# Four small index buffers moved and the routed up-projection matrices padded to 384 columns each, in an S4D, routed-expert, attention and dense-expert block on one Trainium2 core

## The chip, the cores and the metric

The kernel runs on 1 core of a Trainium2 chip. The metric is the device time of one execution in microseconds (us). Before the change the median of 3 runs is 912.46 us (911.31 to 914.74).

## What is computed

The reference, cut to what matters here:

```python
xn = _layernorm(x)                                   # x: (4, 1024, 128)
x = x + _L0_attn_ref(xn, ...) + _L0_ffn_ref(xn, ...) # S4D long convolution + top-2 of 8 experts
xn = _layernorm(x)
x = x + _L1_attn_ref(xn, ...) + _L1_ffn_ref(xn, ...) # attention + 8 dense experts, gated

# _L0_ffn_ref: EMB_DIM 128, HIDDEN 341, 8 experts, TOP_K 2
h1 = einsum('bsd,ehd->bseh', x, W1); h2 = einsum('bsd,ehd->bseh', x, W2)
hidden = silu(h1) * h2
expert_out = einsum('bseh,edh->bsed', hidden, W3)

# _L1_ffn_ref: D 128, FF 512, 8 experts, every token through every expert
h = gelu(einsum('td,edf->etf', x, W1) + b1)
eo = einsum('etf,efd->etd', h, W2) + b2
```

All tensors are float32.

## The kernel before, in words

The program is written by hand: each engine has its own instruction stream, the streams are tied by semaphores, and nothing is ordered by a scheduler. Its stages, by the time of the profile:

1. Up to about 190 us: layer norm, routing of the 4096 tokens to two of eight experts each, the rows scattered to x_slots in device memory, and the S4D kernel and spectra.
2. 190 to 344 us, the routed experts: 19 chunks of 512 slots. For each chunk SyncE loads the expert's split up matrices (`up_load`, L511, tile wc), the down matrices (`down_load`, L514, tile wd) and the rows (`x_load`, L517, tile xc). TensorE turns the rows, multiplies them up (`up`, L1864), down (`down`, L1872) and turns the result back. In between VectorE does the Fourier products of the S4D part.
3. 344 to 384 us: back from the spectra (`positions`, z by prod) and the second layer norm.
4. 384 to 765 us, the dense experts: 8 groups of 512 tokens, 32 units of 128 hidden columns in each (`up1`, `down1`). A unit is six products on TensorE, two activations on ScalarE (L914, L915) and one subtraction on VectorE (L1683).
5. 765 us to the end: attention (`uv`, `scores`, `turn_probabilities`, `attend`).

Where precision is wanted the kernel splits a float32 operand into a high and a low part of type fp32r, and a product becomes three matmuls (`three`, L1766, its matmuls on L1769 to L1771): low by high, high by low, high by high. In a row of the profile `ps<-xt_hi,w_lo` means: the moving operand is xt_hi, the stationary operand (which a weight load puts into the array) is w_lo. The products of z by prod, hid by wd, and the transposes use plain float32.

The up matrices of the routed experts are split once, early: `w0_load` (L485) brings one expert's two matrices side by side to wraw, 128 partitions by WA = 2 * 341 = 682 columns; ScalarE rounds them into the high part of wc (`w0_high`), VectorE subtracts for the low part (`w0_low`, L1199), SyncE stores both to w0_split (L497). In wc each of two buffers holds high and low, 682 columns each, and in each of these the second matrix begins at column HID0 = 341. `up` takes pieces of 128, 128 and 85 columns of each matrix.

Buffers are laid one behind the other in SBUF in the order of their declaration, each rounded up to 32 bytes; a stage's buffers are given back when the stage ends, and later ones reuse the place. One piece of 128 fp32r columns is 512 bytes, so every slice that a product takes of a buffer begins at the same remainder modulo 512 bytes as the buffer, unless the buffer has rows that are no multiple of 512 bytes. From the declarations, the byte address modulo 512 in the kernel before:

```
w_hi, w_lo (dense experts, stationary)                    416
xt1_hi, xt1_lo, hid1_hi, hid1_lo (dense experts, moving)   32
xct_hi, xct_lo (routed up, moving)                        416
wc, buffer 0: high 32 / 372, low 200 / 28  (first / second matrix; stationary)
wc, buffer 1: high 368 / 196, low 24 / 364
hid (routed down, moving) 416; wd (stationary)            192
u_hi, u_lo (scores, moving) 416; xt1 (stationary)          32
pt_hi, pt_lo (attend, moving)                             416
v_hi, v_lo (attend, stationary)                           416
z (moving) and prod (stationary)                          256
ws_hi 128, ws_lo 192
```

The four index buffers next_row, next_gate, row_of and gate_of (32 bytes each, 128 together; GpSimd copies to and from them once per chunk) stand between yo and wst1 among the chunk buffers, so what is declared behind them lies 128 bytes further than what is declared ahead.

Of the kernel before, what the change touches and what calls it, by code (L numbers as in the profile page):

```python
# [16 lines left out]
P = 128  # L17
# [3 lines left out]
HID0 = 341  # L21
J0 = -(-HID0 // P)
# [6 lines left out]


NC = (2 * B * L - E) // W + E
WA, WD = 2 * HID0, J0 * P
MIN_PAIRS, MAX_PAIRS = (2 * B * L // W - 2) // 2, (NC - 3) // 2
SURE = 3 + 2 * MIN_PAIRS
assert NC % 2 == 1
# [55 lines left out]
def program(nc, x, state_params, log_dt, skip, ln_w, ln_b, wg0, w0, lag_row, prefix,  # L91
            dft_fwd, dft_inv, wqk_t, wv, wg1, gate_bias, w1_1, b1, w2_1, b2, out):
    ctx = ExitStack()
    with ctx:
        def sb(name, shape, dt=F32):
            return ctx.enter_context(nc.sbuf_tensor(name, shape, dt))
# [31 lines left out]
        mid1 = sb("mid1", [P, 3, T])  # L128
        mid1_mv = sb("mid1_mv", [P, T, 2])
        shift_col = sb("shift_col", [P, 1])  # L130


        phase = ExitStack()

        def tmp(name, shape, dt=F32):
            return phase.enter_context(nc.sbuf_tensor(name, shape, dt))
# [44 lines left out]
        hid = tmp("hid", [P, J0, W])  # L181
        yt = tmp("yt", [P, W])
        yo = tmp("yo", [P, 2, 4, P])
        next_row = tmp("next_row", [P, 2, 4], mybir.dt.int32)
        next_gate = tmp("next_gate", [P, 2, 4])
        row_of = tmp("row_of", [P, 2, 4], mybir.dt.int32)
        gate_of = tmp("gate_of", [P, 2, 4])
        wst1 = tmp("wst1", [P, STAGES, W])
        chunk_buffers, phase = phase, ExitStack()

# [1573 lines left out]
        def _(pe):  # L1764
            mm = nc.tensor.matmul

            def three(dst, a_hi, a_lo, b_hi, b_lo, first=True, last=True):

                mm(dst, a_lo, b_hi, start=first, stop=False)  # L1769
                mm(dst, a_hi, b_lo, start=False, stop=False)  # L1770
                return mm(dst, a_hi, b_hi, start=False, stop=last)  # L1771
# [92 lines left out]
            def up(q, s, j):  # L1864

                f, r = width0(j), (s + j) % 2
                for bank, col in ((r, 0), (2 + r, HID0)):
                    w = slice(col + j * P, col + j * P + f)
                    last = three(ps[0:f, bank], wc[:, s, 0, w], wc[:, s, 1, w], xct_hi[:, s], xct_lo[:, s])
                last.then_inc(up_done, 1)  # L1870
# [20 lines left out]
            def chunk_products(q, k, s, left, turn):  # L1891
                pe.wait_ge(hid_done, q * J0 + 1)
                up(q, s, 2)
                if not is_first(q):
                    turn_outputs(q - 1)
                down(q, k, s, 0)
                if left:
                    pe.wait_ge(hid_done, q * J0 + 2)
                    pe.wait_ge(xct_lo_done, q + 2)
                    pe.wait_ge(w_up_in[1 - s], (k + s + 1) * 16)  # L1900
                    up(q + 1, 1 - s, 0)
                down(q, k, s, 1)
                if left:
                    pe.wait_ge(hid_done, q * J0 + 3)
                    up(q + 1, 1 - s, 1)
                if left >= 2:
                    turn_inputs(q + 2, k + 1, s)
                down(q, k, s, 2)
# [246 lines left out]
def layout(a):  # L2155

    def by_state(p):

        return p.reshape(2, HH, N).transpose(0, 2, 1).reshape(P, HH)

    freq = np.concatenate([np.arange(0, HF, 2), np.arange(1, HF, 2)]) + 0.5
    place = np.arange(C).reshape(2, P, 2).transpose(2, 0, 1).ravel()
    angle = 2 * np.pi * np.outer(place, freq) / (2 * C)
    dft = np.stack([np.cos(angle), -np.sin(angle)]).astype(np.float32)
    fwd = dft.reshape(2, CT, P, HF).transpose(2, 1, 0, 3)
    inv = dft.transpose(0, 2, 1).reshape(2, HM, P, C).transpose(2, 1, 0, 3)
    tile, expert = np.divmod(np.arange(T * E), E)
    earlier = (tile[:, None] < tile) & (expert[:, None] == expert)
    prefix = np.concatenate([earlier, expert[:, None] == np.arange(E)], 1).astype(np.float32)
    d = dict(  # L2170
        x=a["L0_attn_x"],
        state_params=np.stack([by_state(a["L0_attn_" + n]) for n in ("log_A_real", "A_imag", "C_re", "C_im")], 1),
        log_dt=a["L0_attn_log_dt"], skip=a["L0_attn_D"], ln_w=a["L0_attn_ln_w"], ln_b=a["L0_attn_ln_b"],
        wg0=a["L0_ffn_Wg"].T,
        w0=np.concatenate([
            a["L0_ffn_W1"].transpose(0, 2, 1), a["L0_ffn_W2"].transpose(0, 2, 1),
            np.pad(a["L0_ffn_W3"].transpose(0, 2, 1), ((0, 0), (0, J0 * P - HID0), (0, 0)))
            .reshape(E, J0, P, P).transpose(0, 2, 1, 3).reshape(E, P, J0 * P)], 2),
        lag_row=np.concatenate([np.arange(LO), 2 ** np.arange(NB), E - np.arange(E), np.tril(np.ones((E, E))).ravel()]).astype(np.float32),
        prefix=prefix.reshape(2, P, T * E + E).transpose(1, 0, 2),  # L2180
        dft_fwd=fwd, dft_inv=inv,
        wqk_t=np.stack([a["L1_attn_W_query"].T, a["L1_attn_W_key"].T], 1),
        wv=a["L1_attn_W_value"],
        wg1=np.pad(np.concatenate([a["L1_ffn_Wg"], a["L1_ffn_Wt"]], 1), ((0, 0), (0, GW - E - 1))),
        gate_bias=np.pad(np.concatenate([a["L1_ffn_bg"], a["L1_ffn_bt"]]), (0, GW - E - 1)),
        w1_1=a["L1_ffn_W1"],
        b1=a["L1_ffn_b1"].reshape(E * J1, P).T,
        w2_1=a["L1_ffn_W2"],
        b2=a["L1_ffn_b2"].T,
    )  # L2190
    return {n: np.ascontiguousarray(v) for n, v in d.items()}
```

## Time and profile before

| what | value |
|---|---|
| median of 3 runs | 912.46 us (911.31 to 914.74) |
| the profiled execution's own time | 913.24 us |
| its span (first to last instruction) | 911.1 us |
| mean granted TensorE clock over the span | 0.928 of full speed |
| TensorE busy (PE) | 800.2 us, 88% |
| VectorE busy (DVE) | 642.5 us, 71% |
| ScalarE busy (ACT) | 573.1 us, 63% |
| GpSimd busy (POOL) | 184.3 us, 20% |
| moved by DMA | 82.16 MB |

The profiled execution lies 0.78 us above the median and 2.14 us above its own span. Matmuls overlap: a matmul's recorded duration (some 0.4 us for 512 columns) is longer than the time until the next one starts, so the cost of one matmul in a full stream is the distance between two starts, which the timeline shows. The granted clock is 1.00 for 2.4 GHz and 0.50 for 1.2 GHz.

### The profile page before, as it was taken

To read this page: it belongs to the slowest core of one execution; us is meant where nothing else is said; L and a number is where in the kernel's file an instruction comes from. 1 tells how busy PE (TensorE), PEld (TensorE's weight loads), DVE (VectorE), ACT (ScalarE), POOL (GpSimd) and SP (SyncE) were. 2 spreads that over 40 slices of the span, in tenths; PEclk is the share of its full clock that TensorE was granted. 3 is DMA by queue.
4 is the path that set the end of the run, shared out by engine and by line. 5 is a ranking of instruction groups with operands and counts; after the bars stand their busy time and mean duration, and the time that the engine had idled before them with its cause. 6 is when DMAs were issued, how large, how long until landed. Compare 5 with 4: busy or idle time off the path is not lost.

```text
span 911.1 us, 11973 instructions
## 1 busy us (share of the span) xinstructions
PE 800.2 (88%) x4082; PEld 620.1 (68%) x4082; DVE 642.5 (71%) x1472; ACT 573.1 (63%) x1022; POOL 184.3 (20%) x246
## 2 busy tenths in 40 slices
PE   6964317569999999699999999999999998999998
PEld 6522207446666664377788788878888887899997
DVE  6699205278885485696997889777777775877875
ACT  5840102125555554698987998799898986665564
POOL 0077770006776574000100000000000000000000
PEclk9976555779999999799999999999999999999999
DMA  8534325217777653132441121112121210000000
GB/s 265 204 133 140 122 76 159 66 43 230 230 244 217 195 184 104 23 85 55 102 81 39 37 58 47 40 42 49 47 46 47 47 47 0 8 18 12 19 18 24
DMA packets 79466, 82.16 MB, mean 90 GB/s; under 512 B 11248, under 2 KB 63728, under 8 KB 79152
## 3 DMA queue, kind: packets, MB, share of 16 engines
q1 hardware_dynamic: 68688, 67.98, 26.1%
q0 software_dynamic: 6496, 12.92, 5.5%
q10 hardware_dynamic: 4224, 0.52, 0.4%
q8 instruction: 32, 0.52, 0.2%
q14 instruction: 26, 0.21, 0.1%
HBM read 57.69 MB, written 23.70 MB: 89 GB/s over the span
## 4 chain that ended last, share of the span: by engine, by line
PE 56%; ACT 3%; DVE 3%; POOL 1%; issue 1%; DVEq 0%; ACTq 0%; POOLq 0%
PE ps L1769 17%; PE ps L1771 16%; PE ps L1770 16%; PE ps L2090 3%; PE ps L1954 3%; POOL y_rows L675 1%; ACT hid L914 0%; DVE hid_lo L1683 0%; PE ps L2116 0%; ACT L914 0%; ACT L892 0%; ACT hid_hi L915 0%; PE ps L1935 0%; ACT xn L885 0%; DVE stats L1410 0%
## 5 line engine op out<-in xcount | busy, mean ns | idle before, releaser
L1683 DVE TENSOR_TENSOR hid_lo<-hid,hid_hi 128x512 fp32r<-128x512 f32 x256 | 176.4, 690 | 76.9 <-ACT hid_hi L915 69.5
L914 ACT ACTIVATE hid<-ps,b_sb 128x512 f32<-128x512 f32 x256 | 177.7, 694 | 44.4 <-PE ps L1771 17.5
L915 ACT ACTIVATE hid_hi<-ps,b_sb 128x512 fp32r<-128x512 f32 x256 | 175.6, 686 | 0.0
L1769 PE MATMUL ps<-xt_hi,w_lo 128*128 128x512 f32 x256 | 104.3, 408 | 0.0
L1769 PE MATMUL ps<-hid_hi,w_lo 128*128 128x512 f32 x256 | 101.4, 396 | 1.9 <-DVE hid_lo L1683 1.8
L1771 PE MATMUL ps<-xt_hi,w_hi 128*128 128x512 f32 x256 | 102.1, 399 | 0.0
L1770 PE MATMUL ps<-hid_lo,w_hi 128*128 128x512 f32 x256 | 101.6, 397 | 0.0
L1770 PE MATMUL ps<-xt_lo,w_hi 128*128 128x512 f32 x256 | 100.9, 394 | 0.0
L1771 PE MATMUL ps<-hid_hi,w_hi 128*128 128x512 f32 x256 | 100.6, 393 | 0.0
L675 POOL DMA_INDIRECT y_rows<-yo,row_of x76 | 80.9, 1064 | 71.3 <-issue 66.9
L633 POOL DMA_INDIRECT x_slots<-xn,slot x64 | 68.1, 1063 | 63.3 <-DVE expert_of L1190 44.2
L720 ACT ACTIVATE prod<-ps 128x512 f32<-128x512 f32 (+1 forms) x18 | 10.5, 591 | 95.1 <-remote 63.6
L1769 PE MATMUL ps<-xct_hi,wc 128*128 128x512 f32 (+1 forms) x114 | 66.2, 581 | 3.3 <-DMA wc<-w_split 2.3
L1293 DVE TENSOR_TENSOR hid<-act,ps 128x512 f32<-128x512 f32 (+1 forms) x57 | 39.0, 684 | 39.9 <-ACT act L831 35.5
L831 ACT ACTIVATE act<-ps 128x512 f32<-128x512 f32 (+1 forms) x57 | 34.1, 598 | 52.5 <-PE ps L1771 42.6
L1769 PEld LDWEIGHTS ps<-hid_hi,w_lo 128*128 128x128 f32 x256 | 48.1, 188 | 16.0 <-DVE hid_lo L1683 5.5
L1879 PE MATMUL ps<-hid,wd 128*128 128x512 f32 (+1 forms) x114 | 58.0, 593 | 0.0
L1771 PEld LDWEIGHTS ps<-xt_hi,w_hi 128*128 128x128 f32 x256 | 48.4, 189 | 12.1
L1769 PEld LDWEIGHTS ps<-xt_hi,w_lo 128*128 128x128 f32 x256 | 48.6, 190 | 11.5
L1770 PEld LDWEIGHTS ps<-hid_lo,w_hi 128*128 128x128 f32 x256 | 48.1, 188 | 11.7
L1771 PEld LDWEIGHTS ps<-hid_hi,w_hi 128*128 128x128 f32 x256 | 48.1, 188 | 11.0
L1770 PEld LDWEIGHTS ps<-xt_lo,w_hi 128*128 128x128 f32 x256 | 48.6, 190 | 10.0
(332 smaller groups left out, 1720.2 us busy)
## 6 DMA issues: line engine op xcount, KB each, us to landing
gate_row<-gates_dram SPq DMA_DIRECT2D x64, 256.0 KB, 4.9
wc<-w_split SPq DMA_DIRECT2D x19, 682.0 KB
x_slots<-prod SPq DMA_DIRECT2D x11, 520.0 KB, 10.9
w_split<-wc SPq DMA_DIRECT2D x8, 682.0 KB
xc<-x_slots SPq DMA_DIRECT2D x19, 260.0 KB
wst<-w SPq DMA_DIRECT2D x16, 256.0 KB
wd<-w SPq DMA_DIRECT2D x19, 192.0 KB
acc<-y_rows POOLq DMA_DIRECT2D x14, 256.0 KB, 4.9
```

Source lines behind the costliest of these rows:

```text
L633: nc.gpsimd.indirect_dma_start(x_slots, bass.IndirectOffsetOnAxis(ap=slot[:, k, t:t + 1], axis=0), xn[:, t], None).then_inc(signal, 16)
L675: nc.gpsimd.indirect_dma_start(y_rows, bass.IndirectOffsetOnAxis(ap=row_of[:, s, t:t + 1], axis=0), yo[:, s, t], None).then_inc(y_stored[s ...
L831: nc.scalar.activation(act[0:f, r], ps[0:f, r], ACT.Silu).then_inc(act_done, 1)
L914: nc.scalar.activation(hid1[:, u % 4], ps[:, u % 4], ACT.Gelu_apprx_tanh, bias=b1_sb[:, u:u + 1])
L915: nc.scalar.activation(hid1_hi[:, u % 4], ps[:, u % 4], ACT.Gelu_apprx_tanh, bias=b1_sb[:, u:u + 1]).then_inc(hid1_done, 1)
L1293: tt(hid[0:f, j], act[0:f, r], ps[0:f, 2 + r], mul).then_inc(hid_done, 1)
L1683: tt(hid1_lo[:, u % 4], hid1[:, u % 4], hid1_hi[:, u % 4].bitcast(F32), sub).then_inc(hid1_lo_done, 1)
L1769: mm(dst, a_lo, b_hi, start=first, stop=False)
L1770: mm(dst, a_hi, b_lo, start=False, stop=False)
L1771: return mm(dst, a_hi, b_hi, start=False, stop=last)
L1879: last = mm(ps[:, 4], wd[0:f, s, j * P:(j + 1) * P], hid[0:f, j], start=(j == 0), stop=(j == J0 - 1))
L1954: last = mm(ps[:, g % 4], inv[:, m, part_, t * P:(t + 1) * P], z[:, m + HM * (t // 2), c, part_], start=(m == 0 and part_ == 0), stop=(m = ...
```

## The change

- The four index buffers are declared with the buffers that live through the whole program, ahead of all stage buffers, and no longer behind yo. Every stage buffer ahead of wst1 so lies 128 bytes further than before, and wst1 and wc lie where they did.
- Each of the two up matrices is padded from 341 to 384 columns with zeros in the input array: WA becomes 768 columns, the second matrix begins at column 384 (HALF0), and wc, wraw, w0_split and the rows of the input w0 grow with it. A row of w0 for one expert and partition grows from 1066 to 1152 floats.
- The products keep their sizes: `up` still takes 128, 128 and 85 columns.

Byte addresses modulo 512 after the change:

```
w_hi, w_lo, xt1_hi, xt1_lo, hid1_hi, hid1_lo               32
xct_hi, xct_lo, hid, wd                                    32
wc, both buffers, high and low, both matrices              32
u_hi, u_lo, v_hi, v_lo, pt_hi, pt_lo                       32
z and prod                                                 96
ws_hi 128, ws_lo 192 (as before)
```

The order of instructions on every engine is the same before and after. The instructions that change are the eight ScalarE copies and the eight VectorE subtractions of `w0_high` and `w0_low` (682 to 768 columns), the eight DMAs to wraw (341 to 384 KB), the eight stores to w0_split and the 19 loads of wc (682 to 768 KB each). Apart from these only addresses differ.

```diff
 NC = (2 * B * L - E) // W + E
-WA, WD = 2 * HID0, J0 * P
+HALF0 = J0 * P
+WA, WD = 2 * HALF0, J0 * P
...
         shift_col = sb("shift_col", [P, 1])
+        next_row = sb("next_row", [P, 2, 4], mybir.dt.int32)
+        next_gate = sb("next_gate", [P, 2, 4])
+        row_of = sb("row_of", [P, 2, 4], mybir.dt.int32)
+        gate_of = sb("gate_of", [P, 2, 4])
...
         yo = tmp("yo", [P, 2, 4, P])
-        next_row = tmp("next_row", [P, 2, 4], mybir.dt.int32)
-        next_gate = tmp("next_gate", [P, 2, 4])
-        row_of = tmp("row_of", [P, 2, 4], mybir.dt.int32)
-        gate_of = tmp("gate_of", [P, 2, 4])
         wst1 = tmp("wst1", [P, STAGES, W])
...
                 f, r = width0(j), (s + j) % 2
-                for bank, col in ((r, 0), (2 + r, HID0)):
+                for bank, col in ((r, 0), (2 + r, HALF0)):
                     w = slice(col + j * P, col + j * P + f)
...
         w0=np.concatenate([
-            a["L0_ffn_W1"].transpose(0, 2, 1), a["L0_ffn_W2"].transpose(0, 2, 1),
+            *(np.pad(a["L0_ffn_" + n].transpose(0, 2, 1), ((0, 0), (0, 0), (0, HALF0 - HID0))) for n in ("W1", "W2")),
             np.pad(a["L0_ffn_W3"].transpose(0, 2, 1), ((0, 0), (0, J0 * P - HID0), (0, 0)))
             .reshape(E, J0, P, P).transpose(0, 2, 1, 3).reshape(E, P, J0 * P)], 2),
```

## Rows read from the trace of the kernel before

**Rows 1.** The page: engines' busy time, and the granted clock in 40 slices.
```profile
PE 800.2 (88%) x4082; PEld 620.1 (68%) x4082; DVE 642.5 (71%) x1472; ACT 573.1 (63%) x1022; POOL 184.3 (20%) x246
...
PEclk9976555779999999799999999999999999999999
```

**Rows 2.** Stretches: start:end length, busy us (instructions) per engine, granted clock, DMA, GB/s.
```profile
240.00:300.00 60.00, 56.67 (x236) 36.72 (x235) 42.82 (x69) 32.35 (x72) 42.03 (x60) 1.00 0.78 231
300.00:344.00 44.00, 41.85 (x172) 27.12 (x171) 26.72 (x43) 23.84 (x55) 27.92 (x44) 1.00 0.63 193
...
384.00:765.00 381.00, 379.05 (x1688) 305.18 (x1688) 300.36 (x595) 332.80 (x529) 8.64 (x10) 1.00 0.24 52
765.00:911.10 146.10, 138.78 (x982) 126.40 (x982) 104.09 (x210) 84.21 (x160) 0.00 (x0) 0.99 0.05 15
```

**Rows 3.** The page: the chain that ended last, shares by engine.
```profile
PE 56%; ACT 3%; DVE 3%; POOL 1%; issue 1%; DVEq 0%; ACTq 0%; POOLq 0%
```

**Rows 4.** TensorE's waits from 380 to 766 us: us in total, times, longest.
```profile
PE ps L1769 <- DVE hid_lo L1683: 1.8, 4, 0.7
```

**Rows 5.** Timeline, dense experts, one unit of six products: start us, duration us, instruction.
```profile
700.39 0.40 PE L1769 MATMUL ps<-xt_hi,w_lo 128*128 128x512 f32 x1
...
701.79 0.40 PE L1769 MATMUL ps<-xt_hi,w_lo 128*128 128x512 f32 x1
```

**Rows 6.** Timeline, routed up at the start of its stage, six products apart.
```profile
192.59 0.63 PE L1769 MATMUL ps<-xct_hi,wc 128*128 128x512 f32 x1
...
195.15 0.63 PE L1769 MATMUL ps<-xct_hi,wc 128*128 128x512 f32 x1
```

**Rows 7.** The chain from 344 to 380 us: start us, us, what.
```profile
344.45 24.05 PE ps L1954 x56
```

**Rows 8.** Timeline, routed up of two neighbouring chunks, four products apart in each.
```profile
304.48 0.39 PE L1770 MATMUL ps<-xct_lo,wc 128*128 128x512 f32 x1
...
305.41 0.40 PE L1771 MATMUL ps<-xct_hi,wc 128*128 128x512 f32 x1
...
312.15 0.39 PE L1770 MATMUL ps<-xct_lo,wc 128*128 128x512 f32 x1
...
313.08 0.40 PE L1771 MATMUL ps<-xct_hi,wc 128*128 128x512 f32 x1
```

**Rows 9.** Timeline, attend, nine products apart.
```profile
851.77 0.29 PE L1771 MATMUL ps<-pt_hi,v_hi 128*128 128x256 f32 x1
...
852.85 0.28 PE L1771 MATMUL ps<-pt_hi,v_hi 128*128 128x256 f32 x1
```

**Rows 10.** Timeline, gate logits with 10 moving columns, nine products apart.
```profile
414.71 0.25 PE L1771 MATMUL ps<-ws_hi,xt_hi 128*128 128x10 f32 x1
...
415.71 0.25 PE L1771 MATMUL ps<-ws_hi,xt_hi 128*128 128x10 f32 x1
```

**Rows 11.** Tile wc: duration ns min/median/max, first and last start; who waited for it.
```profile
L720 ACT ACTIVATE wc<-wraw x8: 757/764/774, 43.8 to 144.5; 128x682 fp32r<-128x682 f32 x8
L1199 DVE TENSOR_TENSOR wc<-wraw,wc x8: 860/862/869, 55.7 to 145.5; 128x682 fp32r<-128x682 f32 x8
...
  PE ps L1769: 2.3, 2
```

**Rows 12.** The same operations at 512 columns: tile khat, and the page's costliest groups.
```profile
L720 ACT ACTIVATE khat<-ps x4: 597/597/598, 171.6 to 177.2; 128x512 f32<-128x512 f32 x4
...
L1683 DVE TENSOR_TENSOR hid_lo<-hid,hid_hi 128x512 fp32r<-128x512 f32 x256 | 176.4, 690 | 76.9 <-ACT hid_hi L915 69.5
```

**Rows 13.** Waits up to 190 us: us in total, times, longest.
```profile
PE ps L1834 <- DVE high L1272: 6.2, 1, 6.2
```

**Rows 14.** DMA issues of wc, count and KB each.
```profile
wc<-w_split SPq DMA_DIRECT2D x19, 682.0 KB
```

**Rows 15.** Timeline of ScalarE, dense experts, four activations apart.
```profile
600.93 0.69 ACT L914 ACTIVATE hid<-ps,b_sb 128x512 f32<-128x512 f32 x1
...
603.21 0.72 ACT L914 ACTIVATE hid<-ps,b_sb 128x512 f32<-128x512 f32 x1
```

## The prediction

> **What bounds the kernel now.** I read the page first, then the stretches, the chain, the waits, and last the timeline. The page gives TensorE 800.2 us of 911.1, and a clock at or near full speed from the dense experts on [rows 1]. The stretches show where that holds: 379.05 busy of 381.00 us in the dense experts, 138.78 of 146.10 in attention, some 95% in the routed experts [rows 2]. The chain that ended last has 56% on TensorE [rows 3], and in the dense experts TensorE waits 1.8 us for its partner [rows 4]. So from about 200 us on nanoseconds per matmul are the kernel's time, and the question is what a matmul costs above its columns.
>
> The timeline tells that by distances between starts. In the dense experts six products take 701.79 - 700.39 = 1.40 us, 233.3 ns each [rows 5]. The same kind of product at the granted 1.2 GHz takes (195.15 - 192.59)/6 = 426.7 ns [rows 6], which is 512 columns at one per cycle and nothing else. At 2.4 GHz that would be 213.3 ns. **Each fp32r product of 512 columns thus pays 20.0 ns over its stream, at the high clock only.** Plain float32 hardly pays: z by prod, 24.05/56 = 429.5 ns [rows 7], is two streams of 213.3 and 2.9 ns. Something in the fp32r stream, perhaps the reading of two operands at once from SBUF, costs 20 ns. The change can win only if that depends on how the two addresses stand to each other modulo 512.
>
> **The change part by part.**
>
> *Addresses.* What the 20 ns do with the remainder is shown by two places. Routed up [rows 8]: neighbouring chunks use the two buffers of wc, whose pieces lie at 372, 200, 28 and 368, 196, 24, 364 and so on against a moving operand at 416. That makes eight differences. Four products take 0.93 us in both, 232.5 ns each, as many as in the dense experts with their one difference of 384. So among unequal remainders it makes no difference which. Equal ones are different ground: of the fp32r products only attend has them today, at 416 and 416, with 256 columns. Nine take 1.08 us, 120.0 ns each [rows 9]; the stream is 256/2.4 = 106.7, the excess 13.3 ns. Its other floor is the weight load: with 10 columns a product still takes (415.71 - 414.71)/9 = 111.1 ns [rows 10]. So equal addresses do not bring attend to either floor, it is 8.9 ns above the higher one. I can't read from this whether its 13.3 is a smaller sum per product than 20.0 or a larger one per column. The products whose remainders become equal and which lie on TensorE's full stretches are 1536 in the dense experts, about 300 of the 342 in routed up (the first chunks are waited for), and 192 in the scores: 2028. Attend keeps equal remainders, at 32. The bounds: down to 213.3 + 1.5 (half of z by prod's 429.5 is 214.8), a gain of 18.5 ns, 2028 x 18.5 = 37.5 us; up, the excess of attend per column, 13.3 x 2 = 26.7 ns against 20.0, a loss of 6.7 ns or 13.6 us. I take 0, because the row nearest in kind and size, routed up against the dense experts, changes its difference and not its time, and because attend with equal addresses still pays.
>
> The Trainium skill (TensorE: Matmul & The Clock Gate, Part 2, step 1) says that TensorE has two independent SBUF read ports, one for the moving operand and one for weight loads, and that loading the next tile's weights does not steal from the running matmul. By that rule no remainder can matter and this term is 0, as I take it. The trace agrees in that eight differences cost the same, but not in the rest: the same page (Wait — 56ns, not 53.3ns?) has 512 columns at 215.7 ns, and the dense experts show 233.3 [rows 5]. If the 17.6 ns between came from a conflict that the page leaves out, the whole gain would be open.
>
> *Early splitting, 8 copies and 8 subtractions with 86 more columns.* ScalarE: (764 - 597)/(682 - 512) = 0.98 ns a column [rows 11, 12], so 84 ns more each. VectorE: (862 - 690)/170 = 1.01, so 87 ns more each. ScalarE idles around them. The first two subtractions stand on VectorE ahead of the tables that TensorE waits 6.2 us for [rows 13]: +0.17 us. The other six I cost at nothing, since VectorE idles next to four of them and TensorE is slowed by issue, not by tables, behind the other two; without that cover they cost 6 x 0.087 = 0.5 us.
>
> *More bytes.* 8 loads grow by 43 KB, 8 stores and 19 loads by 86 KB each [rows 14]. At the 231 GB/s of the busiest stretch [rows 2] 86 KB are 0.38 us. Before the chunks that is 8 x 0.19 + 8 x 0.38 + 2 x 0.38 = 5.3 us of transfer in all, from none to all of it on the way; I take 0.4 us, one transfer's lateness, since the transfers have gaps and the route to the first chunk runs over the S4D kernel. In the chunks the load of wc is issued when a chunk's last up product is done and needed more than a chunk later; TensorE waited for it twice, 2.3 us in all [rows 11]. Each of these two grows by 0.38: +0.8 us. The other end is that all 17 are late by it, 6.5 us. The DMA engines are busy to 0.78 in that stretch and go to about 0.82, not full.
>
> A sentence apart: the Trainium skill (DMA: Bandwidth & Descriptors, How a descriptor splits into AXI transactions) says that a transaction must begin at a multiple of 256 bytes and that a descriptor which doesn't start there fetches bytes it won't use. A row of 5456 bytes starts off such a multiple in most partitions, one of 6144 never, so by that page the loads would grow by 7 to 9% rather than 12.6%, and the 0.8 us by some 0.3 less. No run here shows it yet.
>
> *Index buffers.* Copies of 4 elements on GpSimd at another address: nothing, in either direction.
>
> Sum: 913.24 (the profiled execution) + 0 + 0.17 + 0.4 + 0.8 = 914.6; the median lies 0.78 lower: **913.8 us**, where a measurement of this kernel can tell about 0.5% (4.6 us) from no change.
>
> **The rivals.**
>
> *Equal remainders save a part (faster).* Then attend's 13.3 ns is the price of a product with equal remainders, whatever its columns, and 20.0 falls by 6.7 ns: 2028 x 6.7 = 13.6 us, 900.2 us. If only attend's 8.9 ns over its weight load counted, 11.1 ns would go, 22.5 us, 891.3. For it: 13.3 is less than 20.0, and the excess appears only at the high clock [rows 6], as it would where SBUF reads are the limit. Against: eight unequal differences, some within 52 bytes of equal (364 and 368 against 416), show no slope.
>
> *They save all of it (faster).* 37.5 us, 876.3. ScalarE would allow it: four activations in 2.28 us [rows 15] make 1.14 us a unit, less than 6 x 214.8 = 1.29. Against it is attend, which has equal remainders and an excess.
>
> *Equal remainders are the worst case (slower).* Both reads of a matmul then begin at the same place of the interleave, and attend's 13.3 ns at 256 columns become 26.7 at 512: +6.7 ns on each of the 2028, +13.6 us, 927.4. It decides from the point where the price grows with the columns. For it: attend pays 5.2 ns per 100 columns, the dense experts 3.9. Against: attend's weight load of 111.1 ns explains a part of its excess without any conflict.
>
> *The bytes come late (slower).* The wc loads run out of slack, all 5.3 + 6.5 us show: 913.8 + 4.9 + 5.7 = 924.4 at the most, some 919 if half does. Against: two waits in 19 loads.
>
> *The change doesn't do what it says.* The remainders are arithmetic on the declarations, so I give this nothing; a part of the products (gate logits and uv, with ws at 128 and 192) stays unequal, but has 216 matmuls and is left out of all cases.
>
> **How the numbers follow.** No effect of the addresses: 0.47, with its own range 911 to 918.5. A part saved: 0.31. All saved: 0.05. Worst case: 0.12. Late bytes: 0.05. Faster by over 0.5% is 0.31 + 0.05 = 0.36; slower 0.12 + 0.05 = 0.17; the same 0.47. The range takes in the first two with their ends and half of the late bytes, 890 to 920, and leaves out 0.05 + 0.12 + 0.02 = 0.19.
>
> **What the profile after would show.** If I am right, six products of a dense unit still take 1.40 us, the copies read some 848 ns and the subtractions 949, and the wait for wc grows from 2.3 to about 3 us. If a part is saved, a unit takes 1.36 us and the dense stretch is 10 us shorter; if equal is worst, 1.44 us. Attend must stay at 120.0 ns in every case but one: if it moves too, the effect is not the equality of remainders but the absolute address, 32 in place of 416, and my reading of attend as a witness for equality falls with it. A longer stretch before 190 us would be the bytes.

## The result, and the profile after

The changed kernel takes 906.19 us (median of 4 runs, 905.31 to 907.3) against 912.1 us before (4 runs, 911.31 to 914.74): a ratio of 0.9927, 95% interval 0.9908 to 0.9946. It is 0.7% or 5.9 us faster. The forecast was no change, 913.8 us; the time lies in the range of 890 to 920 and on the side that had 0.36.

The page of the changed kernel, whose profiled execution took 906.6 us: span, busy time, granted clock in 40 slices, the chain's shares, one group, one DMA row.

```profile
span 904.5 us, 11973 instructions
...
PE 794.2 (88%) x4082; PEld 621.3 (69%) x4082; DVE 643.0 (71%) x1472; ACT 574.0 (63%) x1022; POOL 183.9 (20%) x246
...
PEclk9976555769999999889999999999999999999999
...
PE 56%; ACT 3%; DVE 2%; POOL 1%; issue 1%; DVEq 0%; ACTq 0%; POOLq 0%
...
L1770 PE MATMUL ps<-xct_hi,wc 128*128 128x512 f32 (+1 forms) x114 | 65.7, 576 | 2.7 <-DMA wc<-w_split 2.5
...
wc<-w_split SPq DMA_DIRECT2D x19, 768.0 KB
```

Against [rows 1, 3] nothing changes places: the same count of instructions, the same 56% of the chain on TensorE. TensorE alone is 6.0 us less busy (800.2 to 794.2). The loads of wc have their 768 KB [rows 14].

Where it went, first by stretches of the changed kernel (columns as in [rows 2]):

```profile
240.00:300.00 60.00, 57.29 (x239) 36.85 (x238) 42.56 (x69) 32.72 (x73) 41.94 (x62) 1.00 0.80 244
...
384.00:757.00 373.00, 371.02 (x1686) 305.54 (x1686) 298.85 (x594) 332.50 (x527) 8.61 (x10) 0.99 0.25 53
757.00:904.50 147.50, 140.05 (x987) 127.08 (x985) 105.21 (x211) 84.68 (x161) 0.00 (x0) 1.00 0.05 15
```

The dense experts do the 1686 matmuls of [rows 2] (there 1688 in 381 us) in 373 us; attention takes what it took. Exactly, by the first product of the stage and the last start of the type that ends it. In the kernel before, the timeline row of the first product:

```profile
384.19 0.77 PE L1769 MATMUL ps<-xt_hi,w_lo 128*128 128x512 f32 x1
```

and tile w_hi (minimum/median/maximum in ns, first and last start in us):

```profile
L1771 PE MATMUL ps<-hid_hi,w_hi x256: 389/392/404, 389.6 to 763.1; 128*128 128x512 f32 x128
```

In the changed one, the same two:

```profile
384.55 0.77 PE L1770 MATMUL ps<-xt_hi,w_lo 128*128 128x512 f32 x1
```

```profile
L1772 PE MATMUL ps<-hid_hi,w_hi x256: 388/389/398, 390.4 to 756.3; 128*128 128x512 f32 x128
```

That is 379.0 us before and 371.8 after. **The dense experts win 7.2 us, and the whole span 6.6.** The rest is small and of both signs. The routed up products start at 190.8 in place of 191.2 us and take, to the start of the last one, 146.3 in place of 147.0; what follows up to the dense experts takes 47.4 in place of 46.0; attention and the end 148.2 in place of 148.0. The sum is -0.4 - 0.7 + 1.4 - 7.2 + 0.2 = -6.7.

What a product costs shows in a settled stretch, as the distance between two starts 60 products apart. Before:

```profile
459.61 0.40 PE L1769 MATMUL ps<-xt_hi,w_lo 128*128 128x512 f32 x1
...
473.61 0.40 PE L1769 MATMUL ps<-xt_hi,w_lo 128*128 128x512 f32 x1
```

After:

```profile
459.19 0.39 PE L1770 MATMUL ps<-xt_hi,w_lo 128*128 128x512 f32 x1
...
472.79 0.39 PE L1770 MATMUL ps<-xt_hi,w_lo 128*128 128x512 f32 x1
```

14.00 us against 13.60: **233.3 ns fall to 226.7**. The excess over the stream of 213.3 ns falls from 20.0 to 13.4 ns, and is not gone.

The low price is not there from a run's first product. The timeline of the changed kernel where a plain float32 transpose (ident, gates) has broken the run of fp32r products:

```profile
435.44 0.27 PE L1943 MATMUL ps<-ident,gates 128*64 128x128 f32 x1
435.47 0.48 PE L1770 MATMUL ps<-xt_hi,w_lo 128*128 128x512 f32 x1
435.79 0.40 PE L1771 MATMUL ps<-xt_lo,w_hi 128*128 128x512 f32 x1
...
436.94 0.39 PE L1770 MATMUL ps<-xt_hi,w_lo 128*128 128x512 f32 x1
...
438.30 0.39 PE L1770 MATMUL ps<-xt_hi,w_lo 128*128 128x512 f32 x1
...
441.02 0.39 PE L1770 MATMUL ps<-xt_hi,w_lo 128*128 128x512 f32 x1
```

The five from 435.79 to 436.94 take 230 ns each, the six to 438.30 226.7, the twelve to 441.02 again 226.7. Averaged over all breaks of the dense experts' stream the changed kernel has 232.7 ns in the first three intervals, 229.8 and 228.1 in the next two triples and 226.7 from the tenth product on; the kernel before has 230.9, 234.6, 231.8 and 233.2.

A break need not be a plain float32 matmul. The gate logits are fp32r products too, with 10 columns, and behind them the changed kernel starts dear again:

```profile
416.01 0.25 PE L1772 MATMUL ps<-ws_hi,xt_hi 128*128 128x10 f32 x1
416.12 0.49 PE L1770 MATMUL ps<-xt_hi,w_lo 128*128 128x512 f32 x1
416.44 0.40 PE L1771 MATMUL ps<-xt_lo,w_hi 128*128 128x512 f32 x1
...
417.84 0.39 PE L1771 MATMUL ps<-xt_lo,w_hi 128*128 128x512 f32 x1
```

Six distances in 1.40 us, 233.3 ns. Behind a wait of TensorE for hid_lo it is the same: 231 to 234 ns in the first three distances, 226.5 in the tenth. So what seems to count is how many products of 512 columns have followed each other without a gap.

Of the distances between dense products 1182 stand beyond the ninth of such a run: 1182 x 6.67 = 7.9 us, about the 7.2 won. The full balance is this: the mean distance of all neighbouring dense products, slow and waiting ones left out, falls from 233.0 to 227.4 ns, 8.2 us over 1457 of them. Some 0.5 us of it is lost in the stage's first fifteen products, more of which the changed kernel runs at the low clock, with starts 427 ns apart (6.12 us in place of 5.64), and 0.5 in the waits for hid_lo and at the stage's end, where a distance of 1140 ns becomes 1294 and one of 740 becomes 855.

So the products that come in short runs gain little. Over the last four distances of each run of six, a routed up product falls from 232.2 to 230.9 ns and one of the scores from 231.7 to 231.3. Routed up stands between plain float32 products. The scores mostly don't: 30 of their 32 runs come straight behind fp32r products of 256 or fewer columns, as here in the changed kernel behind attend:

```profile
785.36 0.28 PE L1772 MATMUL ps<-pt_hi,v_hi 128*128 128x256 f32 x1
785.48 0.40 PE L1770 MATMUL ps<-u_hi,xt_lo 128*128 128x512 f32 x1
...
786.64 0.39 PE L1772 MATMUL ps<-u_hi,xt_hi 128*128 128x512 f32 x1
```

Five distances in 1.16 us, 232 ns, with equal remainders and twelve fp32r products just before. Attend takes 119.0 and 119.5 ns on the mean, hid by wd 431.1 and 431.2.

Tile wc in the changed kernel shows the price of the padding:

```profile
L721 ACT ACTIVATE wc<-wraw x8: 827/838/846, 43.2 to 142.8; 128x768 fp32r<-128x768 f32 x8
L1200 DVE TENSOR_TENSOR wc<-wraw,wc x8: 949/950/957, 55.0 to 143.8; 128x768 fp32r<-128x768 f32 x8
```

The copies grew from 764 to 838 ns, the subtractions from 862 to 950 [rows 11], and the last subtraction still starts earlier than before (143.8, before 145.5).

Last, a loss that nobody ordered. At the end of the routed experts TensorE waits 2.2 us for yt, in both kernels. Before (the last number is the idle time before the row):

```profile
343.79 0.66 PE L1888 MATMUL ps<-ident,yt 128*128 128x128 f32 x4 [2.15 <-ACT yt L835]
```

and the 6 us around it, with columns as in [rows 2]:

```profile
340.00:346.00 6.00, 3.85 (x12) 1.64 (x11) 0.69 (x1) 2.24 (x6) 3.56 (x5) 1.00 0.69 259
```

After:

```profile
342.68 1.11 PE L1889 MATMUL ps<-ident,yt 128*128 128x128 f32 x4 [2.16 <-ACT yt L836]
```

```profile
340.00:346.00 6.00, 3.84 (x10) 1.97 (x9) 0.69 (x1) 2.24 (x6) 3.38 (x5) 0.72 0.52 180
```

The granted clock is 1.00 in these 6 us before and 0.72 after: once the wait is over the changed kernel runs at 1.2 GHz for a while. The transposes take 1.11 in place of 0.66 us, and z by prod behind them 28.7 in place of 27.6: 1.5 us in all, more than the 0.7 that the routed experts had gained.

### The profile page after: what moved, and what is told of

The parts are those of the page before. It is cut to its first block, busy times and chain, and to the rows that moved or that the text cites. A ratio compares the mean times of both kernels' runs of the same rounds, so it can differ in the third digit from the quotient of the medians.

```text
span 904.5 us, 11973 instructions
## 1 busy us (share of the span) xinstructions
PE 794.2 (88%) x4082; PEld 621.3 (69%) x4082; DVE 643.0 (71%) x1472; ACT 574.0 (63%) x1022; POOL 183.9 (20%) x246
## 4 chain that ended last, share of the span: by engine, by line
PE 56%; ACT 3%; DVE 2%; POOL 1%; issue 1%; DVEq 0%; ACTq 0%; POOLq 0%
PE ps L1770 17%; PE ps L1772 16%; PE ps L1771 16%; PE ps L2091 3%; PE ps L1955 3%; POOL y_rows L676 1%; ACT hid L915 1%; DVE hid_lo L1684 0%; ACT hid_hi L916 0%; PE ps L2117 0%; ACT L915 0%; ACT L893 0%; PE ps L1936 0%; ACT xn L886 0%; DVE stats L1411 0%
## 5 line engine op out<-in xcount | busy, mean ns | idle before, releaser
L1771 PE MATMUL ps<-hid_lo,w_hi 128*128 128x512 f32 x256 | 99.7, 389 | 0.0
L1835 PE MATMUL ps<-low,high 64*32 64x32 f32 x256 | 30.7, 236 | 30.0 <-issue 23.9
```

What stands on the lines that cost most here:

```text
L1835: mm(o, high[states, 0, c * CH + h], low[states, 0, c * CH + h], start=True, stop=False)
```

## The experiments

Two theories stood after the result. One: equal remainders make a product cheaper. The other: the absolute place does it (the weights went from 416 to 32), or some part of the change other than the dense experts' addresses. All ratios are against the kernel before on the same chip, with 95% intervals. The first four ran on a chip where the kernel before takes 872.04 us (14 runs, 868.85 to 873.31): its routed experts begin about 40 us earlier, the rest is alike, so only comparisons among the four and with that number are made. Stage lengths are from the first to the last start, as above.

**e1: the index buffers moved, no padding.**

```diff
+        next_row = sb("next_row", [P, 2, 4], mybir.dt.int32)
...
-        next_row = tmp("next_row", [P, 2, 4], mybir.dt.int32)
```

> Only the index buffers are moved; the up matrices stay at 682 columns. The dense experts' and the attention's operands all lie at 32, the routed up pieces stay unequal. Theory A (equal remainders of the moving and the stationary operand shorten long streams of fp32r products, so only the dense experts gain): dense stretch 372 us as after the change, steady 226.7 ns per product, time 905 to 906. Theory B (the padding, through the routed up, brings part of the gain): 908 or more.

865.51 us (863.94 to 866.39), ratio 0.9933 (0.9911 to 0.9956). Its timeline, 60 products apart:

```profile
418.72 0.39 PE L1769 MATMUL ps<-xt_hi,w_lo 128*128 128x512 f32 x1
...
432.32 0.39 PE L1769 MATMUL ps<-xt_hi,w_lo 128*128 128x512 f32 x1
```

13.60 us, 226.7 ns, and a dense stage of 371.4 us. The move of 128 bytes alone gives the whole gain.

**e2: the padding, the index buffers where they were.**

```diff
-WA, WD = 2 * HID0, J0 * P
+HALF0 = J0 * P
+WA, WD = 2 * HALF0, J0 * P
```

> Only the padding to 384 columns; the index buffers stay, so w at 416 against 32 in the dense experts as before. Theory A: dense stretch 379 us, 233.3 ns per product, and the time is 912 plus the price of the bytes, 912 to 914. Theory B: below 911.

874.04 us (872.76 to 877.43), ratio 1.0037 (1.002 to 1.0054). Sixty products take 13.95 us, 232.5 ns, the dense stage 378.4. The padding gives nothing and costs: the interval puts it at 1.7 to 4.7 us, the medians lie 2.0 apart. Of this its profile shows, against that of e1, 1.6 us before the first chunk (152.4 against 150.8) and 0.7 us in the routed experts.

**e3: the kernel before, with a gap of 384 bytes ahead of the dense experts' moving buffers.** Weights stay at 416, the moving operands come to 416 too.

```diff
+        gap1 = tmp("gap1", [P, 96])
         xt1_hi = tmp("xt1_hi", [P, G, W], F32R)
```

> The kernel before with a gap of 384 bytes ahead of xt1_hi: the dense experts' moving operands lie at 416, as w does. Equality as the cause: dense stretch 372 us, 226.7 ns, time 905. The absolute place as the cause (w at 32 is good, at 416 bad): 379 us, 233.3 ns, time 912.

864.46 us (864.07 to 865.79), ratio 0.9928 (0.9899 to 0.9957). Sixty products from 417.18 to 430.78 us, 226.7 ns; dense stage 371.5. The absolute place is out: both at 32 (e1, the changed kernel) and both at 416 are cheap, one at each is dear. So is a clash of one operand with some third buffer that stayed where it was: in this stage e1 moves the stationary operand alone and e3 the moving ones alone, and both win the same. It is the difference of the two addresses, and one unused buffer does what the change does. (The gap also moves hid1, the unrounded buffer that stands between the moving ones.)

**e4: the same with a gap of 128 bytes**, moving minus stationary 256 modulo 512.

> The kernel before with a gap of 128 bytes ahead of xt1_hi: moving operands at 160, w at 416, a difference of 256 in place of 128. If equality alone counts: 379 us and 233 ns, time 912. If the price goes with the difference, another steady distance than 233.3, between 226.7 and 240 ns, and a dense stretch between 371 and 390 us.

863.47 us, ratio 0.9914 (0.9886 to 0.9942). Its timeline:

```profile
416.21 0.39 PE L1770 MATMUL ps<-xt_hi,w_lo 128*128 128x512 f32 x1
...
429.81 0.39 PE L1770 MATMUL ps<-xt_hi,w_lo 128*128 128x512 f32 x1
```

226.7 ns again. So equality modulo 512 isn't the condition either; a difference of 256 does as well. From here on each difference is tried at one place only, with the stationary operand at 416.

**e5, e6, e7, e9, e10: gaps of 448, 352, 256, 64 and 416 bytes**, for differences of 64, 480, 384, 192 and 32. These ran on chips where the kernel before takes 913.54 (e5 to e8) and 913.05 us (e9 to e12).

> A gap of 448 bytes: moving at 480, stationary at 416, difference 64. If the price grows with the distance from a multiple of 256: between 226.7 and 233.3 ns, some 230, dense stretch 375 us. If only 128 modulo 256 is bad: 226.7 ns and 372 us. If every difference that is no multiple of 256 is bad: 233 ns and 379 us.

> A gap of 352 bytes: moving at 384, stationary at 416, difference 480 (-32), so that the two also stand at different places of a 64-byte block. If only multiples of 128 or 256 matter: 226.7 ns or a value between, 372 to 375 us. If the place within 64 bytes matters by itself: another steady distance than at 64, possibly above 233 ns or below 226.7.

> The kernel before with a gap of 256 bytes ahead of xt1_hi: dense moving operands at 288, w at 416, moving less stationary = 384 modulo 512 (-128). So far 0 and 256 gave 226.7 ns and 128 gave 233.3. If the remainder modulo 256 decides, 384 is as bad as 128: 233 ns, dense stretch 379 us, same time as before. If 128 alone is bad (a direction): 226.7 ns, 372 us, 0.8% faster.

> A gap of 64 bytes ahead of xt1_hi: moving at 96, stationary at 416, difference 192. Measured so far, steady ns: 0 and 256 226.7, 64 228.9, 128 and 384 233, 480 233.3. If the price repeats every 256 bytes and is the same on both sides, 192 is as 64: 229 ns, dense stretch 374.5 us. If it repeats but is not symmetric, 192 lies with its neighbours 128 and 480 (which is 224 modulo 256): 233 ns, 379 us.

> A gap of 416 bytes: moving at 448, stationary at 416, difference 32. If a start off the stationary operand's 64-byte grid is dear by itself, as 480 was: 233 ns, 379 us. If the price rises from 0 over 64 to 128: between 226.7 and 228.9 ns, some 373 us.

| kernel | moving - stationary, mod 512 | ns a product, over one settled stretch of 60 | dense stage, us | ratio |
|---|---|---|---|---|
| e3, e1, changed | 0 | 226.7 | 371.4 to 371.8 | 0.9928, 0.9933, 0.9927 |
| e10 | 32 | 233.3 | 379.2 | 1.0008 (0.9995 to 1.002) |
| e5 | 64 | 228.9 | 374.4 | 0.9923 (0.9906 to 0.994) |
| before | 128 | 233.3 | 379.0 | 1 |
| e9 | 192 | 233.3 | 380.1 | 1.0018 (1.0002 to 1.0034) |
| e4 | 256 | 226.7 | 372.0 | 0.9914 |
| e7 | 384 | 232.5 | 379.4 | 0.9979 (0.9956 to 1.0003) |
| e6 | 480 | 233.3 | 379.3 | 1.001 (0.9983 to 1.0037) |

The one between, e5, as its timeline has it:

```profile
460.42 0.39 PE L1770 MATMUL ps<-xt_hi,w_lo 128*128 128x512 f32 x1
...
474.15 0.39 PE L1770 MATMUL ps<-xt_hi,w_lo 128*128 128x512 f32 x1
```

13.73 us, 228.9 ns. Two differences give the full gain, 64 two thirds of it, and the rest none: a step of 32 bytes to either side of equal loses everything. The 232.5 of 384 is its stretch; over all products beyond the ninth it has 233.0, and before 233.2. What sets 64 apart is the stage's length and not the ratio, whose interval covers that of the full gain. No distance from a multiple of 256 orders the table: 32 costs more than 64, and 192, which is 64 below 256, more than 64 itself. As 320 and 448 weren't tried, the rule behind it stays open.

**e8: the changed kernel, with two chunks' up pieces next to each other.** If a run has to be longer than nine products to settle, twelve in a row should show it in the routed experts.

```diff
                     pe.wait_ge(w_up_in[1 - s], (k + s + 1) * 16)
-                    up(q + 1, 1 - s, 0)
                 down(q, k, s, 1)
+                if left:
+                    up(q + 1, 1 - s, 0)
```

> The changed kernel with the second down product of a chunk ahead of the first up piece of the next, so that two up pieces, 12 fp32r products, follow each other without a plain float32 product between. If a stream must run some 9 products before it settles at 226.7 ns, products 10 to 12 of these runs take 227 ns, where products of runs of six take 231 on average; gain at most 19 x 25 ns = 0.5 us, so the time is that of the changed kernel within what can be measured. If the routed products are slow for another reason (their DMA load, their addresses), all 12 stay at 231 to 233 ns.

904.26 us (902.45 to 907.4), ratio 0.9902 (0.9877 to 0.9928). The end of one run of twelve in its timeline:

```profile
301.42 0.39 PE L1770 MATMUL ps<-xct_hi,wc 128*128 128x512 f32 x1
301.65 0.39 PE L1771 MATMUL ps<-xct_lo,wc 128*128 128x512 f32 x1
...
302.56 0.39 PE L1772 MATMUL ps<-xct_hi,wc 128*128 128x512 f32 x1
302.79 0.60 PE L1862 MATMUL ps<-ident,xc 128*128 128x128 f32 x4
```

Four products in 0.91 us, 227.5 ns. By place in the runs of twelve the means are 228 to 231 ns behind the second to fifth product, then 230.2, 229.0, 227.4, 227.5, 226.8 and 226.7 behind the eleventh. The routed up products do follow the remainders, once their run is long enough.

**e11: the same order of work, index buffers moved, but no padding**, so that wc's pieces keep their many remainders.

> Move only (no padding) with the up pieces of a chunk in runs of 12 products. The routed up matrices lie at mixed remainders. If products 7 to 12 of a run shorten through the equal remainders alone, here they stay at 231 to 233 ns, where the padded kernel in the same order had 226.7 to 227.5. Time: the padding's gain in routed up is at most 0.5 us and its bytes cost up to 3 us, so this is level with or faster than the change itself, ratio to before 0.990 to 0.993.

902.05 us (901.14 to 907.0), ratio 0.9904 (0.9871 to 0.9937). The end of a run of twelve:

```profile
316.17 0.40 PE L1771 MATMUL ps<-xct_hi,wc 128*128 128x512 f32 x1
...
316.63 0.40 PE L1770 MATMUL ps<-xct_lo,wc 128*128 128x512 f32 x1
316.87 0.39 PE L1771 MATMUL ps<-xct_hi,wc 128*128 128x512 f32 x1
317.10 0.60 PE L1861 MATMUL ps<-ident,xc 128*128 128x128 f32 x4
```

Places seven to eleven stay at 229 to 239 ns, 232.9 on the mean, where e8 has 227.5: without equal remainders a run of twelve doesn't settle at the low price. Still the kernel isn't slower than e8. TensorE's waits between 186 and 345 us say why. e8 (us in total, times, longest):

```profile
PE ps L1889 <- ACT yt L836: 1.4, 1, 1.4
PE ps L1880 <- DMA wc<-w_split: 1.0, 2, 0.8
PE ps L1880 <- DVE hid L1294: 0.4, 1, 0.4
```

e11:

```profile
PE ps L1861 <- DVE xct_lo L1288: 11.9, 1, 11.9
PE ps L1888 <- ACT yt L835: 1.4, 1, 1.4
```

The wait ahead of the stage, 11.9 us, is the same in both. With the padding two waits for wc, 1.0 us together, and one of 0.4 are left, without it none; the routed experts take 145.0 us in e8 and 143.7 in e11. What the equal remainders give there the larger loads take back. In both the wait for yt is 1.4 us, not 2.2, the clock stays at 1.00 behind it, and the way to the dense experts takes 45.2 us in both in place of 47.4. The two intervals lie on each other, and that of e12 below reaches into both, so none of the three is shown to be the fastest; the medians of e8 and e11 are the lowest.

**e12: the changed kernel again**, on the chip of e9 to e11.

> The changed kernel once more, beside the others on one chip: ratio to before 0.993. If the padding's bytes cost what e2 showed (0.37%), it is slower than the kernel that only moves the buffers, in which the order of the up pieces gains at most 0.5 us, by 2 to 3 us; if they cost nothing on this chip, the two are level.

905.98 us (903.35 to 906.62), ratio 0.9919 (0.9896 to 0.9943), the dense stage as before. The low clock behind the wait for yt comes again (1.11 us for the transposes). It isn't the change's own mark, however: e5, the kernel before with one gap, shows it too (0.76 in the same 6 us), and in e1 and e10 it falls too (0.87 from 299 to 305 us, 0.78 from 346 to 352) and z by prod takes 1.7 us more than in the kernel before. In e2, e3, e4, e6, e7 and e9 the clock stays at 1.00 behind the same wait of 2.1 to 2.2 us. What decides was not found. As e1 has the low clock and e3 has not, and both win in the dense experts, it is no part of that gain.

## Why the prediction was wrong

**The step that failed** is the term of the addresses, set at 0 "because the row nearest in kind and size, routed up against the dense experts, changes its difference and not its time, and because attend with equal addresses still pays". It is -7.2 us in the dense experts, and e1 and e3 show that the addresses alone bring it.

*Routed up was no witness* [rows 8]. Its products come six between plain float32 matmuls, and a run of six hardly settles even at equal remainders. The changed kernel has these there and still 230.9 ns; only with twelve in a row (e8) do they pay less. Eight differences with one time so told of the run length, not of the addresses. The dense experts in turn had one difference (384, stationary minus moving, which is 128 the other way round), and the map has it among those that gain nothing. "Some within 52 bytes of equal show no slope" was true and worthless twice: the stage hid any slope, and e10 shows that 32 bytes off already pays in full.

*Attend was half a witness* [rows 9]. Its 13.3 ns over the stream at 256 columns, read as the price of a product with equal remainders whatever its columns, gave 6.7 ns a product for the rival of a part saved. Measured are 13.4 ns at 512 columns and 6.67 saved: the size was right for a settled product. Whether the agreement is more than luck isn't shown, since attend too stands in runs of its own and its weight load of 111.1 ns lies close.

*The count was wrong in the rival.* It gave 2028 products the whole gain, 900.2 us. Only 1182 dense ones have it, and the 342 and 192 of the other two stages nearly nothing, since both come in runs of six. With that count the rival says 913.2 - 7.9 + 1.4 for the bytes and the copies, less 0.8 to the median: 905.9 us, against 906.19 measured. That it comes so close is in part luck: the 1.4 did not show in the changed kernel, and the 1.5 us of the clock behind yt are not in it.

*All saved, and equal is worst:* neither. A price above the low one remains even where the remainders are equal, and none of the eight differences tried costs more than 233.3 ns in its settled stretch.

*The copies and subtractions* were foretold at 848 and 949 ns and took 838 and 950. The 0.17 us that two of them should cost before the chunks, and the 0.4 us for early bytes, do not show in the changed kernel (its first chunk is 0.4 us earlier); e2's profile has 1.6 us there on another chip. *The waits for wc* were to grow from 2.3 to 3.1 us and came to 2.5 [rows 11], 2.1 in e12. The padding as a whole is worth -1.4 us in the forecast, -1.7 to -4.7 us in e2, and nothing that e1 and the changed kernel can tell apart (0.9933 and 0.9927).

*The loads' growth of 7 to 9%*, given beside the 12.6% of the bytes, is not what the trace has. Of the packets that each carry one row of wc, the median took 209 ns before (5456 bytes) and 234 after (6144), 12% more. The figure was also small for its own premise, by which it comes to 10%: with starts spread evenly over the multiples of 16 bytes, an old row fetches 120 bytes too many on the mean. The sum didn't use it.

*The index buffers as such* cost nothing, as foretold. *The clock behind the wait for yt*, 1.5 us, stood in no case.

*The rule of the Trainium skill.* I put the weight of no effect on the trace, with a rule of the same sign beside it: the Trainium skill (TensorE: Matmul & The Clock Gate, Part 2, step 1) has two independent read ports in SBUF, and weight loads that don't steal from the running matmul. The measurement decides here: e3 moves only the dense experts' buffers on the moving side, and 233.3 ns become 226.7. The prediction had the right doubt in its hands, the 17.6 ns between the 215.7 of the Trainium skill (the same page, Wait — 56ns, not 53.3ns?) and the trace's 233.3 [rows 5], and then let two poor witnesses settle it. That the two operands' reads meet in SBUF is the explanation I would give, but it is argued, not shown. No run tells whether the moving operand meets its own weights or the load of the next ones.

## What to carry to other kernels

Where a stretch consists of long runs of fp32r products and each start lies some 20 ns above the columns, try the difference of the two operands' addresses first: a gap of one small unused buffer cost nothing and was worth 0.7% here, at differences of 0 or 256 modulo 512, while 32 bytes beside equal gave nothing. Before a stage is taken as evidence that a quantity doesn't matter, look whether it is in the regime in which the quantity could show; here a run of 512-column products had to be longer than about nine. And keep the free part of a change (the move) apart from the part with a price (the padding): only the first had earned anything.

## What the runs showed of the hardware that was not expected

- In a settled stretch a product of 512 fp32r columns at 2.4 GHz takes 226.7 ns at address differences of 0 and 256 modulo 512, 228.9 at 64, and 232.5 to 233.3 at 32, 128, 192, 384 and 480.
- The low price comes only some nine products of 512 columns after the last break (232.7 ns, then 229.8, 228.1, 226.7). A plain float32 matmul, an fp32r product of 10 columns and a wait all count as a break, and the scores stay at 231.3 ns behind twelve fp32r products of 256 columns.
- The same wait of 2.2 us leaves the granted clock at 1.00 in some kernels and at 0.72 or 0.76 over the 6 us around it in others; in the changed kernel it fell in both executions profiled (e12). When it falls it costs 1.5 us.
